# Two graph-attention layers in a GNN kernel: edges moved from the free axis to the partitions, with keys and values gathered in one row

## What is computed

```python
recv = segment_sum(edge_attr_128, dst)                     # update
h = relu(concat([recv, x, u]) @ W1 + b1) @ W2 + b2
x = layernorm(x + h)

def tconv(x, Wq, Wk, Wv, We, Ws, ...):                     # attend, twice
    q, k, v = x@Wq+bq, x@Wk+bk, x@Wv+bv                    # (n, 4, 32) each
    e = (edge_weight @ We)                                 # (edges, 4, 32)
    alpha = einsum('ehc,ehc->eh', q[dst], k[src]+e) / sqrt(32)
    amax  = segment_max(alpha, dst)
    ex    = exp(alpha - amax[dst]); denom = segment_sum(ex, dst)
    out   = segment_sum((v[src]+e) * (ex/(denom[dst]+1e-16))[:, :, None], dst)
    return out + x@Ws + bs

h = relu(tconv(x, layer 1)); h = relu(tconv(h, layer 2))
return layernorm(x + h)
```

## Time and profile before

| what | value |
|---|---|
| median of 3 timed runs | 3948.93 us (3940.69 to 3951.46) |
| profiled execution, first to last instruction | 3951.6 us |
| mean granted PE clock | 0.801 of full |
| busy: PE / DVE / ACT / POOL | 2901.8 / 1768.9 / 1423.2 / 2014.0 us |
| HBM traffic | 333.73 MB read, 72.56 MB written |

### The profile page before, as it was taken

The page is one execution under the profiler, slowest core; times in us unless marked ns, Lnnn a source line. Parts: engine busy times, 40 slices in busy tenths (PEclk is TensorE's granted clock), DMA queues, the critical chain, the costliest instruction groups (busy, mean ns, idle before and its releaser), DMA issues. The chain is left out here.

```text
span 3951.6 us, 85365 instructions
## 1 busy us (share of the span) xinstructions
PE 2901.8 (73%) x20525; PEld 2444.9 (62%) x20525; DVE 1768.9 (45%) x5708; ACT 1423.2 (36%) x4457; POOL 2014.0 (51%) x2395
## 2 busy tenths in 40 slices
PE   4666999577777777777777875776777776777777
PEld 3445999466666666666666654665666665666655
DVE  5453445243444444344344872443444343434456
ACT  1001444233333333333333652333333333333357
POOL 5200111355665665566564665655666555665533
PEclk6557999677777877777888996778777777787889
DMA  7895322333333333333333662333333333333320
GB/s 206 269 266 177 85 83 82 85 88 91 90 91 89 90 92 89 90 91 90 89 90 73 155 151 79 90 90 90 91 91 90 90 89 88 92 90 92 87 45 25
DMA packets 527894, 407.14 MB, mean 103 GB/s; under 512 B 195972, under 2 KB 495412, under 8 KB 527464
## 3 DMA queue, kind: packets, MB, share of 16 engines
q1 hardware_dynamic: 413544, 282.02, 24.5%
q0 software_dynamic: 64768, 124.04, 12.9%
q10 hardware_dynamic: 49536, 0.55, 0.7%
HBM read 333.73 MB, written 72.56 MB: 103 GB/s over the span
## 5 line engine op out<-in xcount | busy, mean ns | idle before, releaser
L1359 POOL DMA_INDIRECT a_ring<-xg,edge x1792 | 1690.5, 943 | 1147.1 <-issue 524.3
L1410 PE MATMUL bank<-a_ring,a_weight_t 128*128 128x130 f32 x3584 | 707.2, 351 | 208.4 <-DVE acc_all L1515 178.3
L1497 DVE TENSOR_REDUCE a_bound<-bank 128x4 f32<-128x512 f32 x448 | 308.3, 688 | 1198.1 <-remote 1089.2
L1410 PEld LDWEIGHTS bank<-a_ring,a_weight_t 128*128 128x128 f32 x3584 | 608.5, 246 | 281.0 <-DVE acc_all L1515 230.3
L1515 DVE SCALAR_TENSOR_TENSOR acc_all<-acc_all,a_decay,bank 128x130 f32 x1792 | 627.6, 350 | 323.1 <-issue 46.3
L1373 PE MATMUL bank<-ident,a_ring 128*128 128x128 f32 x1792 | 350.9, 318 | 146.9 <-issue 120.9
L1383 PE MATMUL bank<-a_shared 17*128 17x128 bf16 x1792 | 234.4, 238 | 253.3 <-issue 252.6
L1391 PE MATMUL bank<-a_x_t,a_query 128*128 128x128 f32 x1792 | 336.7, 335 | 92.6 <-issue 74.7
L1464 ACT ACTIVATE a_weight_t<-bank 128x512 f32<-128x512 f32 x448 | 271.6, 606 | 352.2 <-remote 187.0
L1453 ACT ACTIVATE a_x_t<-bank,a_run 128x128 f32<-128x128 f32 x896 | 255.4, 368 | 392.5 <-DVE a_run L1500 276.5
L1391 PEld LDWEIGHTS bank<-a_x_t,a_query 128*128 128x128 f32 x1792 | 279.7, 233 | 151.2 <-issue 108.9
(11 more groups left out here) (276 smaller groups left out, 4063.4 us busy)
## 6 DMA issues: line engine op xcount, KB each, us to landing
a_query<-rec SPq DMA_DIRECT2D x896, 128.0 KB
c_ring<-in_edge_attr SPq DMA_DIRECT2D x344, 192.0 KB
a_ring<-xg,edge POOLq DMA_INDIRECT x1792
rec<-u_q_scores SPq DMA_DIRECT2D x98, 256.0 KB
rec<-p_q_scores SPq DMA_DIRECT2D x98, 256.0 KB
a_shared<-nrows SPq DMA_DIRECT2D x896, 8.5 KB
a_shared<-crows SPq DMA_DIRECT2D x224, 28.0 KB
c_node<-drec ACTq DMA_DIRECT2D x344, 1.5 KB
```

Source lines behind the costliest of these rows:

```text
L1359: pool.indirect_dma_start(out=ring[:, k, t, 0:FEAT], out_offset=None, in_=rows_of[:, :], in_offset=bass.IndirectOffsetOnAxis(ap=tiles_of(k ...
L1410: last = pe.matmul(sum_bank(t), weight_t[k % 2][:, t * P:(t + 1) * P], ring[:, k, t, :], start=True, stop=True)
L1497: dve.tensor_reduce(bound[:, k, :, STEPS - 1:STEPS].rearrange("q t s -> q (t s)"), score_bank(k), AX.X, ALU.max, negate=True).then_inc(max ...
```

## The change

Both attention layers are rewritten, and what feeds them.

- A window is now a group of 128 nodes (49 of them). The tiles of a layer are a fixed 832, in 26 groups of 32 (G), and a step handles a quad of four tiles. Edges stand on partitions.
- The projections make query, key, value and skip rows per node once: queries (132 wide: 128 and 4 for the edge weight) stay in SBUF as three bf16 parts (`q3`); keys and values go to DRAM as one row of 256 f32 (1 KB), and POOL gathers that row per edge.
- DVE builds `hot_t`, the 0/1 matrix (node x edge, bf16), from `places` broadcast to all partitions, 16 tiles at a time. PE multiplies it with the three parts of the queries (three bf16 matmuls of 132 columns per tile), turns it once (bf16), and later sums the weighted values with it (one f32 matmul of 136 columns).
- DVE multiplies queries with keys and reduces to scores per head, multiplies values by their exponentials, and adds sums into `acc`, in place of the maximum per tile.
- Maxima are found once for each group of 32 tiles: scores are turned to (head, tile) x edge, two scans along the edges forwards and backwards, two scans across the tiles on one partition, two more along the edges, all on DVE, with products and turns on PE and copies and exponentials on ACT between them (16 DVE instructions, called links). They run for the group before, in steps 0 to 3 of a group.
- `count_stage` and `collect_stage` make other lists; `update_stage` and `project_stage` end in the projections and the split into three parts; `output_stage` no longer turns and mixes heads.

The core of the diff:

```diff
-        ring = sb("ring", [P, NS, QUAD, RW])
-        query = sb("query", [P, QS, QUAD, FEAT])
+        ring = wide[:, RING:RING + 2 * G * KV].rearrange("p (b t c) -> p b t c", b=2, c=KV)
...
+            def queries(at, later, q):                                   # PE
+                at.wait(multiplied, QUADS, q - 1 + QUADS * later)
+                at.wait(edge_there, QUADS, q - 1 + QUADS * later)
+                for t in range(QUAD):
+                    for s in range(SPLIT):
+                        rows = q3[:, bass.ds(held[q % 2 * QUAD + t], 1), s, :].rearrange("p a c -> p (a c)")
+                        last = pe.matmul(query_out(q)[:, t, :], hot_t[:, b, q * QUAD + t, :], rows, start=(s == 0),
...
+            def sums(at, back, q):
+                at.wait(hot_there, QUADS, q + 1 - QUADS * back)
+                at.wait(weighted, QUADS, q + 1 - QUADS * back)
+                for pair in (0, 1):
+                    at.wait(added, G, (q - 1) * QUAD + 2 * pair + 2 - G * back)
+                    for t in (2 * pair, 2 * pair + 1):
+                        last = pe.matmul(sum_out(t), hot[q % 2][:, t, :], ring[:, (at.b + back) % 2, q * QUAD + t, LEAD:KV],
...
+            def step(at):                                                # POOL
+                for q in range(QUADS):
+                    at.wait(summed, 2 * QUADS, 2 * (q + 1) - 4 * QUADS)
+                    for n in range(q * QUAD, (q + 1) * QUAD):
+                        pool.indirect_dma_start(
+                            out=ring[:, at.b, n, :], out_offset=None, in_=kv[:, :],
...
+            def scores(at, q):                                           # DVE
+                dve.tensor_tensor(product[:, :, :], query_out(q)[:, :, 0:FEAT], ring[:, at.b, here, 0:FEAT], ALU.mult
+                                  ).then_inc(multiplied, 1)
+                dve.tensor_reduce(score[at.b][:, :, here].rearrange("p h t -> p t h"),
+            def weigh(at, back, q):
+                dve.tensor_tensor(values, values, repeat(here[:, :, LEAD:LEAD + HEADS].unsqueeze(3), 3, HC), ALU.mult
+                                  ).then_inc(weighted, 1)
+            def add(at, back, q):
+                    at.wait(added, G, q * QUAD + t - G * back)
+                    here = sums_of(held[q % 2 * QUAD + t])
+                    dve.tensor_tensor(here, here, sum_out(t), ALU.add).then_inc(added, 1)
...
+            def step(at):
+                linking, b = at.has(1), 1 - at.b
+                for s in range(QUADS):
+                    if s == 0 and linking:
+                        add_edges(at, b)
+                    if at.has():
+                        scores(at, s)
+                    if s == 1 and linking:
+                        scan_tiles(at, b)
+                    if s == 2 and linking:
+                        share(at, b)
+                    if s == 2 and at.has():
+                        make_hot(at, 0, 1)
+                    if s == 6 and at.has(-1):
+                        make_hot(at, 1, 0)
+                    back, q = old(s)
+                    if at.has(back):
+                        weigh(at, back, q)
+                    back, q = old((s - 1) % QUADS)
...
+                        add(at, back, q)
+                    if s == LAG and linking:
...
+                        sink_sums(at)
+                    if s == 0 and linking:
+                        scan_lanes(at, b)
+                    if s == 1 and linking:
+                        sink(at, b)
```

The projections (`update_stage`, `project_stage`) and POOL's new part:

```diff
-def query_scores(pe, m, layer, x_cols, score_bank, heads=range(HEADS)):
-def make_terms(dve, chain, m, layer, terms_ps, put):
+def project_wide(pe, m, layer, cols, out):
+    return pe.matmul(out[:, 0:PROJ], cols, m["wall"][layer][:, 0:PROJ], start=True, stop=True)
+def spread_rows(dve, chain, m, layer, g, wide_in, narrow_in, query, pairs):
+    chain(dve.tensor_tensor(query[:, :], wide_in[:, 0:QW], ball[:, 0:QW], ALU.add))
+    chain(dve.tensor_tensor(pairs[:, :], wide_in[:, QW:PROJ], ball[:, QW:PROJ], ALU.add))
+    chain(dve.tensor_tensor(m["skip"][:, bass.ds(g * P, P)], narrow_in, ball[:, PROJ:ALL], ALU.add))
+            def split_rest(g, k):                                        # POOL
+                pool.tensor_tensor(rest[k][:, :], query[k][:, :], part_of(m, g, 0), ALU.subtract).then_inc(left_over, 1)
+            def split_low(g, k):
+                pool.tensor_tensor(part_of(m, g, 2), rest[k][:, :], part_of(m, g, 1), ALU.subtract).then_inc(left_over, 1)
```

More of the change, by code:

```diff
@@ L392, in _ @@
[L392 to L396 removed]
+                                        ).then_inc(fetched, 16)
+            pool.wait_ge(fetched, 16 * CH)
+            for t in range(CH):
+                codes(t)
+            pool.wait_ge(taken, 5)
+            pool.wait_ge(ends, 4)
+            step(pool.memset(cut_row[:, 0:1], 1.0))
+            step(pool.tensor_tensor(cut_row[:, 1:TCAP], first_row[:, 1:TCAP], last_row[:, 0:TCAP - 1], ALU.subtract))
@@ new lines, in grow, with step @@
+            def grow(at, b):
+                at.wait(below_ps, 1, 0)
+                act.activation(ring[:, b, :, LEAD:LEAD + HEADS], grown_out.rearrange("p (h t) -> p t h", h=HEADS), ACT.Exp
+                               ).then_inc(grown, 1)
+            def step(at):
+                linking = at.has(1)
+                for s in range(QUADS):
+                    if at.has():
+                        edge_parts(at, s)
+                    if s == 1 and linking:
+                        enter_columns(at, 1 - at.b)
+                    back, q = after(s)
+                    if at.has(back):
+                        copy_hot(at, back, q)
+                    if s == 1 and linking:
+                        grow(at, 1 - at.b)
@@ L1530, in _ @@
-            dve.memset(run[:, NS - 1, QUAD - 1, STEPS - 1:STEPS], 0.0).then_inc(ready, 1)
-            for s, most in enumerate((BIG, ANEW / 2)):
-                dve.memset(bound[:, :, :, s:s + 1], most).then_inc(ready, 1)
-            dve.wait_ge(ready, 5)
-            dve.wait_ge(list_in, 16)
-            begin = Round(dve, dve.snap(last_tiles(dve, m) * 0))
-            for body in range(SCORE):
-                carry(begin, body)
-                maximum(begin, body)
-            rounds(dve, m, step, None, last_tiles)
+                        at.wait(summed, 2 * QUADS, 2 * q + 1 + t // 2 - 2 * QUADS * back)
```

1702 lines of the change are left out of this document (789 added, 913 removed).

## The result

The changed kernel takes 3883.87 us (median of 4, 3876.53 to 3891.15), the kernel before 3950.19 us beside it: a ratio of 0.9838, interval 0.9817 to 0.9858. So it is faster, as forecast, but by 66 us (1.6%, clear of noise) and not by 674, and lies above the stated range of 3110 to 3680. The profiled execution spans 3883.8 us.

A forecast was written before the change was run, and what follows sets the result against it. Old attention was taken as bound by waits for SP's loads, the new by DVE beside POOL: 26 groups of 42.5 us plus ends made 1144 a layer, twice 2288, plus 988 elsewhere: 3276 us, range 3110 to 3680.

The forecast's parts named there:

- What bounds the kernel: Old attention: bound by waits, 602 us of DVE idle before the maxima, traced to SP's mask and query loads.
- POOL, 40.0 a group: New attention: gathers start 1.25 us apart, 32 per group, a floor of 40.0 us a group, 1040 a layer.
- DVE, 40.5 a group: New attention: DVE's work per group, 32.5 us for quads, 5.8 links, 1.8 `make_hot`, 0.4 register loads.
- 42.5: New attention: forecast us per group, DVE's 40.5 plus 2 for crossings between engines; bounds 40 and 50.
- PE, 22 to 36: New attention: PE needs 22 us a group at full clock, 36 at half, still under DVE's 40.5.
- (d): Rival, attention: PE's register steps not hidden, 0.31 us per query product, kernel 4056 us; break-even 0.29; chance 0.10.
- What lies beside what: New attention: engines' streams overlap; eight link crossings a group, 0.25 us each if not fully covered, 2 us allowed.
- Other stages: Outside attention: lists and edge sums 330 us, update 377, projection 155 plus 3, output 120; 988 in all, for 1074.
- (a): The forecast itself, attention: DVE and POOL side by side, 42.5 us a group, kernel 3200 to 3400; chance 0.50.
- (b): Rival, attention: DVE operations hold off POOL's gather descriptors, 48.8 us a group, 1311 a layer, kernel 3610; chance 0.20.
- (c): Rival, attention: DVE's long loop fetches code at each of 24 jumps back, 60 to 120 us, kernel 3360; chance 0.12.
- (e): Rival: POOL's floor alone bounds attention, all else hidden, side stages leaner, kernel 3110 us; chance 0.08.

The follow-up runs named there:

- Run 8: The kernel before, its attention gathers replaced by plain POOL loads of 128 rows of the same 512 bytes (other rows): 2705 us, ratio 0.6750 to the kernel before.
- run 5: The changed kernel with plain POOL loads for attention gathers (other rows), each followed by an idle 208-column POOL addition: 3377 us, ratio 0.8428 to the kernel before.
- run 12: The changed kernel with the first two of each quad's four gathers replaced by plain POOL loads (half the rows wrong): ratio 0.7896 to the kernel before.

## Why the prediction was wrong

**What bounds the kernel: this step failed.** It read the 602 us ahead of the maxima, released from outside, as waits for SP's loads, and said that the new kernel "removes the transfers waited for". Run 8 shows that the loads were never the bound: without gathers the old attention takes 811 us with the same loads. What the maxima waited for were PE's scores, whose signals came late: 535 of the 602 us passed after PE's records of them had ended. The new attention has the same gathers, and so the same wait: a body of four tiles took 6.40 us, a quad takes 1377/208 = 6.62. What was won in attention, 134 us, is less than the 205 that 16 fewer quads a layer give at the old pace; no wait was removed, and each quad takes longer.

**POOL, 40.0 a group.** The pitch nearly held: a gather 1.00 us busy, the next 0.30 later, 1.30 for 1.25, so the floor is 41.6. It was the missing term beside it, the delay of PE's signals while gathers run, that costs 190 to 290 us a layer.

**DVE, 40.5 a group.** Right in its parts: the three wide operations as priced, `make_hot` 0.743 (0.75 was one end, 0.9 taken), four adds in 1.60 us, so 0.44 apart for 0.49. With every link's wait in it, the whole ran in 38.3 us a group once signals were prompt and POOL was quick, so 42.5 was if anything too long. DVE was busy 58% of the stage, for the 80% that the forecast asked for.

**PE, 22 to 36.** Products stood 0.06 us apart in a full queue (12 in 0.86 us, above) and 0.13 where each waited for its register step (12 in 1.61), below the 0.29 of (d).

**What lies beside what.** The eight crossings were the right place to look and priced wrongly: 0.25 us for a hand-over like the earlier trace rows, where three in five of those out of PE came late, most of them by 1 to 7. The 2 us a group allowed for the links' crossings, with nothing for the hand-overs of every quad, is the term of the sum that was mis-sized: by run 5 the late signals add 7 to 11 us a group (190 to 290 over 26).

**Other stages.** The first: 328 for 330, the last 122 for 120. The update's sum of work was right (364 us once unblocked, 377 forecast), but the two subtractions that are new on POOL stand in no term of its sum, and PE's copy was queued behind one of them and its wait: 138 us. The same in the projection, where its loop of waits was taken as 3.2 us a group and was 3.9; 143 us when reordered.

**Rivals.** (a) is what run 5 shows for the kernel without the delay: 3377 on a slower chip, with the update's 125 us still in it. (b) is real and small: beside `make_hot` a gather took 1.23 us on average (105 gathers of both layers), beside the weighing alone 1.10 (351), beside neither 0.95 (1208). The mean rose from 0.943 to 1.003, not to the 1.22 of 48.8 a group, so the price fell; what held attention up was not POOL's pace, and that 1311 a layer lies near the measured 1377 and 1366 would have been luck. (c) was right in where and how long DVE stands, 59 us at the 20 jumps of both layers, some 31 of it on the path; that code is fetched there is argued, since the runs show only that the stand goes with the jump. The Trainium skill ("Runtime: NRT & Kernel Launch", section "Instruction fetch mechanics") states that a taken branch to code no longer held stalls; the trace agrees, 2.7 to 3.4 us a jump for a DVE loop of 356 rows. On PE the next step follows its jump by 0.06 us, though its loop has some 1149 records; the same section gives PE room for 2048 instructions. (d) and (e) fell. The true cause was among none of them, though its sign was in the trace of before: 5.20 us between the end of PE's scores and their semaphore (run 8).

## What to carry to other kernels

An idle "released from outside" is not a DMA until a run says so: set the producer's end beside the consumer's start, and if the gap is microseconds with nothing between, ask what delays the signal. Before a change is priced by the wait it removes, that wait's supposed cause is best taken away in the old kernel alone, as run 8 did. A new operation on an engine costs what is queued behind its wait; and a hand-over out of PE, in a stage where POOL gathers without a stop, is to be priced in microseconds, so such loops want fewer gathers in a row (run 12 shows what that is worth, on rows that are not the right ones) or more tiles in flight between PE and the others (not tried here).

## What the runs showed of the hardware

- While POOL issues gathers by index one behind the other, PE's completions are seen late, up to 8 us, and held ones often appear together, 0.06 to 0.12 us apart. About two in three of the late ones in the first attention stage appear in a stop of POOL, 0.6 to 2.2 us after its last gather ended (0.74 to 0.92 in the list above); the rest appear while gathers still follow each other, as the 1506.33 above. Same for rows of 512 bytes and 1 KB, in order or scattered. Plain loads by POOL with the same packets show none of it (0 of 861), nor do those of DVE's and ACT's signals that are in the trace.
- It builds up: two gathers and two plain loads in turn leave at most 1.0 us, pauses of 0.2 us between gathers don't help, rows of eight are worse, and the number of signals has no part.
- It is more frequent at PE's full clock (227 of 272) than at half (239 of 487). Why a gather holds PE's completions back, and what the clock does to it, stays open. Room for more sums or turned tiles in PSUM, so that a round trip may last longer, wasn't tried: the free columns lie in banks that other engines read at that time.
